# Another merged order of steps for the second stage of a two-block Perceiver kernel, on VectorE, TensorE and GpSimd

## What is computed

```python
x = x + L1_attn(layernorm(x))    # Q, K, V = x@W + b; softmax(Q K^T / 8) V, per head; @ W_O + b_O
x = x + L1_ffn(layernorm(x))
# L1_ffn: scores = softmax(x @ gate_w.T); the two largest and their experts
#         y = sum over the two of x2 * x3 (three matmuls and a silu of an expert)
#         z = silu(x @ sw1.T) * (x @ sw2.T) @ sw3.T
#         returns y + z
```

## Time and profile before

| | |
|---|---|
| Median of three runs | 3797.93 us (3792.13 to 3812.2) |
| The profiled execution | 3799.34 us |
| Its span | 3797.5 us |
| Second stage within it | about 2400 to 3380 us |
| Mean granted clock of TensorE over the span | 0.89 of full speed |

### The profile page before, as it was taken

One profiled execution on the slowest core, in us unless ns is written; L12 is line 12 of the kernel. 1 busy time (PEld: TensorE's weight loads), 2 busy tenths in 40 slices (PEclk: granted clock), 3 DMA queues, 4 the chain that ended last, 5 costly groups with the idle time before them and its releaser, 6 DMA issues.

```text
span 3797.5 us, 112181 instructions
## 1 busy us (share of the span) xinstructions
PE 2953.9 (78%) x44524; PEld 2280.8 (60%) x44524; DVE 2100.2 (55%) x5626; ACT 1089.7 (29%) x2279; POOL 721.5 (19%) x815
## 2 busy tenths in 40 slices
PE   1778778778778778778778788899999998867763
PEld 1456555555555555555555565677777777756662
DVE  5666666666666666666666665344444444433334
ACT  2333333333333333333333332111111111114431
POOL 4212212212222212212212211111111111102210
PEclk9779889889889989989889888888888888889997
DMA  4111111111111111111111102000000000027777
GB/s 143 34 36 34 33 41 33 33 41 33 33 40 34 33 41 33 36 39 32 42 32 32 46 28 82 13 14 12 12 12 12 12 12 13 16 78 224 226 208 213
DMA packets 105241, 201.38 MB, mean 53 GB/s; under 512 B 13336, under 2 KB 41504, under 8 KB 103968
## 3 DMA queue, kind: packets, MB, share of 16 engines
q1 hardware_dynamic: 93728, 173.85, 15.3%
q0 software_dynamic: 6528, 17.87, 1.2%
q10 hardware_dynamic: 4608, 4.20, 0.3%
HBM read 167.51 MB, written 28.35 MB: 52 GB/s over the span
## 4 chain that ended last, share of the span: by engine, by line
PE 66%; DVE 18%; issue 8%; DMA 4%; ACT 3%; DVEq 0%; SPq 0%; POOL 0%; POOLq 0%; ACTq 0%
PE ps L356 17%; PE ps L1169 9%; PE ps L1241 5%; PE ps L717 4%; PE ps L734 4%; PE ps L1214 3%; PE ps L1496 3%; DVE mem L1073 3%; DVE neg_max L1068 3%; PE ps L713 2%; PE ps L738 2%; DMA y_pairs<-mem,pair_u 2%; PE ps L784 2%; PE ps L1505 2%; PE ps L1234 2%
## 5 line engine op out<-in xcount | busy, mean ns | idle before, releaser
L356 PE MATMUL ps<-mem 128*128 128x32 f16 (+3 forms) x5196 | 473.0, 245 | 40.0 <-DVE mem L1775 36.0
L356 PEld LDWEIGHTS ps<-mem 128*128 128x128 f16 x5196 | 391.0, 98 | 95.1 <-DVE mem L1775 36.1
L1169 PE MATMUL ps<-xt,mem 128*128 128x128 f32 x3072 | 367.5, 278 | 14.7 <-ACT xt L1268 14.7
L1169 PEld LDWEIGHTS ps<-xt,mem 128*128 128x128 f32 x3072 | 352.1, 193 | 24.3 <-ACT xt L1268 22.0
L1073 DVE RECIPROCAL mem<-ps 128x64 f32<-128x64 f32 x256 | 142.5, 557 | 279.3 <-PE ps L738 279.3
L436 POOL TENSOR_TENSOR mem<-mem 128x514 f16<-128x514 f32 x136 | 159.2, 1172 | 561.1 <-ACT mem L431 561.1
L791 ACT ACTIVATE mem<-ps 128x512 f32<-128x512 f32 (+3 forms) x320 | 178.8, 559 | 258.0 <-PE ps L356 129.2
L1089 POOL TENSOR_TENSOR rstd<-var_eps,neg_half 128x1 f32<-128x1 f32 x128 | 70.2, 548 | 865.5 <-DVE var_eps L905 865.5
L850 ACT ACTIVATE mem<-ps 128x512 f32<-128x512 f32 x256 | 152.1, 594 | 284.1 <-PE ps L717 284.1
L1241 PE MATMUL ps<-mem 128*128 128x256 f32 x512 | 198.4, 571 | 44.7 <-DVE mem L1358 44.7
L685 PE MATMUL ps<-mem 64*128 64x257 f32 x1024 | 164.7, 422 | 49.9 <-DVE neg_max L1068 49.9
(11 more groups left out here) (266 smaller groups left out, 5882.8 us busy)
## 6 DMA issues: line engine op xcount, KB each, us to landing
mem<-in_experts SPq DMA_DIRECT2D x72, 512.0 KB, 3.7
mem<-in_ctx_t SPq DMA_DIRECT2D x136, 257.0 KB, 3.6
mem<-in_ctx_n SPq DMA_DIRECT2D x136, 256.0 KB, 2.9
mem<-in_experts SPq DMA_DIRECT2D x72, 259.0 KB, 2.8
mem<-x_sorted SPq DMA_DIRECT2D x72, 128.5 KB, 2.2
mem<-y_pairs SPq DMA_DIRECT2D x32, 256.0 KB, 3.9
x<-in_x_tok SPq DMA_DIRECT2D x34, 128.0 KB, 2.0
x_mid<-x SPq DMA_DIRECT2D x32, 128.0 KB, 1.7
```

Of the source, the lines that this page charges most:

```text
L356: last = pe.matmul(dst, a, b, start=start and i == 0 and j == 0, stop=stop and i == n - 1 and j == 2)
L1169: last = pe.matmul(dst[:, i * P:(i + 1) * P], w2(name, C, n)[:, kc, oc * P:(oc + 1) * P], xt_f[:, kc], start=(kc == 0), stop=(kc == 1))
```

## The change

Three strings of the second stage are replaced by others with the same numbers of `o` and `y`. No instruction is added, removed or given another wait.

```diff
--- before.py
+++ after.py
@@ -180,10 +180,10 @@
         sync=("ooo"),
     ),
     "second": dict(
-        tensor=("oooyyyyyoyoyoyyyoo"),
+        tensor=("oooyyyyyoyyooyyyoo"),
         scalar=("oyoooooyy"),
-        vector=("yyyyooyoooooyoyooooooyyoooooyyooyoyoyooooo"),
-        gpsimd=("yyooo"),
+        vector=("yyyyooyooooooyyyoooooyooooooyoyoyyyooooooo"),
+        gpsimd=("yoyoo"),
         sync=("o"),
     ),
     "third": dict(
```

## The result

The changed kernel is slower. Over 20 runs of each the median is 3830.36 us (3810.86 to 3869.04) against 3806.76 us (3792.13 to 3851.72), a ratio of 1.0068 with the interval [1.0036, 1.01]. The runs of either kernel fall into two groups. Before: 16 of 20 lie from 3792 to 3812 (median 3804.3) and 4 from 3835 to 3852 (3839.5). After: 11 from 3811 to 3833 (3819.3) and 9 from 3851 to 3869 (3854.8). So the change costs 15 us inside either group, 0.4%; the other 9 us between the medians are the group that a run fell into. What is known of the groups stands at the end.

What follows compares the result with a forecast made beforehand. The prediction took TensorE to bound the second stage, with three waits and a slow clock holding each slot at 30.72 us. The moved steps summed to 0 over 31 slots, so it forecast 3798 us, range 3784 to 3814.

Steps and rivals of the forecast that it cites:

- The three waits: TensorE's waits in each second-stage slot: 1.38 us for `o5_f`, 0.88 for `pt5_f`, 0.47 for the transposed x's copy.
- Item 1: TensorE, second stage: scores of group 1 ahead of gate cost 0, between -1.2 and +1.2 us in all.
- Item 2: VectorE: `xn6` fits the gap before `qk5_f` of group 0, cost 0, with 0.97 us more before TensorE needs it.
- Items 3 and 4: VectorE: `qk5_f` of groups 2 and 3 separated, slot-end steps reordered; cost 0, `p5_norm` expected 0.4 us earlier.
- Item 5: POOL: power ahead of `biased5`, which then runs beside `xn6`; cost 0, one delaying the other by 0 to 0.73 us.
- The slot follows the clock: Second-stage slots settle at 30.72 us, taking up 0.5 us on the faster side, at least 0.12 on the slower.
- The sum is 31 x 0 = 0: All moved steps over 31 second-stage slots add 0, with bounds of -1.2 and +1.2 us.
- The rivals: Clock comes loose in second-stage slots: 3774 us, chance 0.07; POOL's power holds up VectorE: 3825 us, chance 0.05.
- The second: VectorE waits for POOL's power before `qk5_f`; slower if the wait is over 1.7 us; 3825 us, chance 0.05.
- forecast of "same": Whole kernel: time within 0.5% (19 us) of before, chance 0.88.

Runs made afterwards that it cites:

- q4: Reduced kernel with only TensorE's string changed and 128 do-nothing instructions at the start of TensorE's program: 1634.97 us.
- r1: Kernel before, reduced: first and third stages cut to 3 trips each, second stage whole, strings of before: 1637.73 us.
- q1: r1 with 128 do-nothing instructions added at the start of TensorE's program: 1628.37 us.
- x1: r1 with one more full-size matmul (0.24 us) for TensorE in each slot: 1660.63 us.
- e1: Whole kernel before with only TensorE's string changed: 3818.97 us, ratio 0.9985 to before.
- e4: Whole kernel before, unchanged, run once more for a second trace: 3839.33 us, ratio 1.0009 to before.
- e3: Whole changed kernel, run once more for a second trace: 3830.76 us, ratio 1.0021 to before.
- r2: Changed kernel with all three new strings, reduced in the same way as r1: 1655.14 us.

## Why the prediction was wrong

- **What bounds the kernel: right in its parts, incomplete.** The three waits stayed at 1.38, 0.88 and 0.47 us. Besides these and the slow clock, another thing that stops TensorE, the supply of its own instructions, was left out. The view of waits had no line for it in the stretch that I read, since the one reload trip of that execution came just behind it, at 3195.
- **Item 1, TensorE's swap: right by itself.** Gate and the scores take 0.85 us together, 0.83 before. With the reloads away q4, r1's strings with this swap, has q1's second stage, 980.4 us.
- **Item 2, `xn6` ahead of `qk5_f`: right.** `qk5_f` of group 0 ends at 2740.92, TensorE needs it at 2738.14 + 2/3 of 5.62 = 2741.89. Of the cover of 0.97 us, as much is still there.
- **Items 3 and 4: right.** No wait for a `qk5_f` or a score appears, and `p5_norm` ends 0.98 us ahead of the transposes in the slot shown, 0.72 before: 0.26 us earlier, where 0.4 was expected.
- **Item 5, two engines at once: its bound held.** `xn6` took 0.81 us beside `biased5` of 0.73, and 0.40 alone: 0.41 us more, between the ends 0 and 0.73. The Trainium skill (SBUF — State Buffer, "SBUF: two separate sides") says that the one that starts first has the shared port pair for its whole instruction, VectorE in some modes only. By that, `xn6` would have ended 0.40 us behind `biased5`, near 2740.5; it ended at 2740.26. So the trace shows such a slowdown, but a smaller one. The cover was enough.
- **"The slot follows the clock": right, and stronger than I used it.** Two pauses of 0.41 us and 30.72 us slots in the same trace show it. But `self5_y` at 6.54 us, behind a slow stretch of 6.8 us, was a trait of one execution (5.1 to 5.4 in ordinary slots of the others, with a stretch of 3.4), and the slower side ends at an edge (x1), which TensorE's string alone reached once (e1).
- **"The sum is 31 x 0 = 0": the step that failed.** It summed what the moved steps cost and took TensorE's instructions to be there at no cost in any order. The missing term is the number of reload trips that the change adds, times 3.1 to 3.4 us in the trace of the changed kernel: 5 more in the profiled executions (21.3 us more from the first branch to the fifteenth), 2 more from e4 to e3 (6.5 us), 3 more from r1 to r2 (10.4 us). The medians moved by 15 us inside the groups of the whole kernel and by 17 in the reduced one.
- **The rivals.** Neither took place. (The second has a slip in its sum: 27.89 + wait + 1.69 reaches 30.72 at a wait of 1.14 us, not 1.7.) The forecast of "same" held nearly everything because each rival was a wait on an engine or the clock. The range was too narrow besides: three runs had shown only the lower group, and the kernel before itself reaches 3852. Even inside the lower group the changed kernel's median, 3819.3, lies above the range.

Shown: the reloads cost the time in the second stage, their number follows where the loop lies against the blocks, and without them the two orders are alike there. **Open:** why another order of equally many instructions makes more trips reload. The loop is as long as before and lies at the same place, so it should turn on when things happen. TensorE's own records don't show it: in r2's trace the last 28 records ahead of the branch take 2.95 to 2.96 us at all 15 branches, whether the next trip reloads or not. And the same kernel has 2 such trips in one execution and, by its times, more in the next.

## What to carry to other kernels

Before an order of steps is compared, look at the instruction queue inside the loops: a steady loop should fetch nothing, and if it fetches, count its blocks (recorded instructions over 256, and where it starts) and shift it until it touches one block fewer (shortening it should do the same, but was not tried). Here 128 instructions that do nothing gave back all that the new order had cost, and 64 of them cost 78 us more. A single profiled execution with one odd "issue" wait in it is a warning about the others.

## What the runs showed of the hardware that I had not expected

- This loop of TensorE, when it touches seven blocks of 256 instructions, fetches none in 14 trips; reaching 7.08 blocks it fetched nine in 1 to 6 of 14, 7.17 in 2 to 11, and 7.33 in all. A trip with a fetch took 2.8 to 7.0 us longer, but for two that took 0.1 and 0.2.
- The 0.41 us pauses inside `o5_ps`, in all traces but the first, whatever the order and wherever the loop lies. Their cause is open.
- A slot that the clock holds at 30.72 us with or without 0.8 us of standing still inside it.
- The two groups of runs, some 35 us apart. In the one trace of a run of the upper group (e3, 3850.87 us) the third stage's matmuls (L1488 to L1510) take 399 us from first to last, at a mean granted clock of 0.91, and 354 to 359 at 0.96 to 0.99 in the seven traces of the lower (the expectation of r1 has 396 and 351 to 356 for the same stage); its view of lines for 3400 to 3760 shows the matmuls of the experts slower, first the changed kernel's lower run, then e3:

```profile
L1496 PE MATMUL ps<-mem 128*128 128x128 f32 x1152 | 146.9, 282 | 1.5 <-DMA mem<-in_experts 1.5
```

```profile
L1496 PE MATMUL ps<-mem 128*128 128x128 f32 x1056 | 150.2, 303 | 1.5 <-DMA mem<-in_experts 1.5
```

That stage has the same code in all of them. Which of its two rhythms a run falls into was not tried.
